# Output weights folded into each batch's key-value sums, and a query that is normalised by token before it is turned

## What is computed

```python
x = x + attn_a(layernorm(x)); x = x + ffn(layernorm(x))
x = x + attn_b(layernorm(x)); x = x + ffn(layernorm(x))

def attn_a(x):                                 # linear attention, 16 heads of 16
    q = elu(x @ Wq + bq) + 1; k = elu(x @ Wk + bk) + 1; v = x @ Wv + bv
    kv  = einsum('bkhd,bkhm->bhdm', k, v)       # sums over a batch's 2048 tokens
    out = einsum('bqhd,bhdm->bqhm', q, kv)
    out = out / maximum(einsum('bqhd,bkhd->bqh', q, k), 1e-6)[..., None]
    return out @ Wo + bo
def ffn(x):
    return square(relu(x @ Ws1)) @ Ws2 + routed # routed is zero unless a weight bound fails
```

## Time and profile before

| | before |
|---|---|
| time, median of 3 runs | 434.23 us (433.89 to 434.29) |
| profiled execution, span | 432.7 us |
| TensorE busy | 416.6 us (96%) |
| VectorE busy | 316.3 us (73%) |
| ScalarE busy | 217.6 us (50%) |
| GpSimd busy | 217.1 us (50%) |

### The profile page before, as it was taken

The page is one execution under the profiler, slowest core; times in us unless marked ns, Lnnn a source line. Parts: engine busy times, 40 slices in busy tenths (PEclk is TensorE's granted clock), DMA queues, the critical chain, the costliest instruction groups (busy, mean ns, idle before and its releaser), DMA issues.

```text
span 432.7 us, 7753 instructions
## 1 busy us (share of the span) xinstructions
PE 416.6 (96%) x2570; PEld 345.7 (80%) x2570; DVE 316.3 (73%) x707; ACT 217.6 (50%) x383; POOL 217.1 (50%) x317
## 2 busy tenths in 40 slices
PE   8998999999999999899999999999999999999993
PEld 5787889988987988889788886787887787787862
DVE  6769977676668766647878887877778767787864
ACT  3766777778777775326434342343244324334341
POOL 3675776776677764031345336534516416514532
PEclk9999999999999999999999999999999999999998
DMA  8701221111100000300110111011001010011103
GB/s 264 245 7 46 57 88 54 51 49 48 48 0 0 2 2 1 101 0 6 51 52 20 36 51 52 2 51 50 21 31 35 18 52 27 26 51 50 50 4 106
DMA packets 22793, 20.59 MB, mean 48 GB/s; under 512 B 3271, under 2 KB 22733, under 8 KB 22733
## 3 DMA queue, kind: packets, MB, share of 16 engines
q1 hardware_dynamic: 22172, 19.32, 14.1%
q10 hardware_dynamic: 560, 0.52, 0.4%
HBM read 11.32 MB, written 8.45 MB: 46 GB/s over the span
## 4 chain that ended last, share of the span: by engine, by line
PE 68%; DVE 8%; ACT 7%; POOL 7%; issue 5%; SPq 2%; DMA 1%; DVEq 1%; POOLq 0%; ACTq 0%
PE PB L1462 7%; PE PT L1504 6%; PE PA L1462 6%; PE PB L1483 6%; PE PA L1538 4%; PE PA L1544 4%; PE PA L1539 3%; PE PT L1548 3%; PE PA L1473 3%; ACT scratch L568 3%; PE PB L1510 3%; POOL ln_rstd L441 2%; PE PG L1334 2%; POOL ln_rstd L439 2%; DVE ln_bn L800 2%
## 5 line engine op out<-in xcount | busy, mean ns | idle before, releaser
L491 POOL TENSOR_TENSOR ln_a<-ln_bn 128x4 f32<-128x4 f32 x32 | 6.5, 203 | 136.1 <-DVE ln_bn L1003 136.1
L463 POOL TENSOR_TENSOR xn_pair<-scratch,xn_pair 128x1024 fp32r<-128x1024 f32 x16 | 38.4, 2402 | 18.9 <-ACT xn_pair L579 18.9
L883 DVE SCALAR_TENSOR_TENSOR scratch<-scratch,PB 128x512 f32<-128x512 f32 x32 | 20.9, 684 | 36.4 <-ACT scratch L615 36.3
L1003 DVE BATCH_NORM_STATS2 ln_bn<-x_all 128x6 f32<-128x256 f32 x128 | 44.9, 412 | 0.9
L568 ACT ACTIVATE scratch<-x_all,ln_shift,ln_rstd 128x255 f32 (+1 forms) x60 | 31.2, 593 | 22.6 <-POOL ln_shift L445 22.6
L452 POOL TENSOR_TENSOR x_all<-x_all,wvo 128x1024 f32 (+1 forms) x16 | 38.6, 2410 | 0.1
L452 POOL TENSOR_TENSOR x_all<-x_all,ob_rows 128x1024 f32<-128x1024 f32 x16 | 37.7, 2356 | 0.0
L1307 PE MATMUL PB<-wk_hi,xt_hi 128*128 128x256 f32 x128 | 36.9, 288 | 0.6 <-DVE xt_lo L828 0.4
L1309 PE MATMUL PB<-wk_hi,xt_lo 128*128 128x256 f32 x128 | 36.2, 283 | 0.0
L1308 PE MATMUL PB<-wk_lo,xt_hi 128*128 128x256 f32 x128 | 36.2, 283 | 0.0
L736 ACT ACTIVATE scratch<-PA,ln_rsq 128x256 f32<-128x256 f32 x30 | 12.6, 471 | 45.4 <-PE PA L1462 40.2
(11 more groups left out here) (247 smaller groups left out, 1139.0 us busy)
## 6 DMA issues: line engine op xcount, KB each, us to landing
x_all<-n_L_attn_a_inputs_q_dram SPq DMA_DIRECT2D x15, 512.0 KB, 3.5
out_dram<-x_all SPq DMA_DIRECT2D x15, 512.0 KB, 3.1
out_dram<-x_all SPq DMA_DIRECT2D x2, 256.0 KB, 2.2
x_all<-n_L_attn_a_inputs_q_dram ACTq DMA_DIRECT2D x2, 128.0 KB, 3.0
x_all<-n_L_attn_a_inputs_q_dram SPq DMA_DIRECT2D x2, 128.0 KB, 2.7
setup<-in_L_attn_a_Wk_dram SPq DMA_DIRECT2D x1, 256.0 KB, 4.6
setup<-in_L_attn_a_Wq_dram ACTq DMA_DIRECT2D x1, 256.0 KB, 5.0
wvo<-in_L_attn_a_Wv_dram SPq DMA_DIRECT2D x1, 256.0 KB, 6.7
```

Of the source, the lines that this page charges most:

```text
L463: nc.gpsimd.tensor_tensor(xn_pair[:, :, 1, :], xn[g % 2], xn_pair[:, :, 0, :].bitcast(F32), ALU.subtract).then_inc(x_lo, 1)
L1003: nc.vector.bn_stats(ln_bn[:, slot, t:t + 1, :], x_tile(n, t)).then_inc(bn, 1)
```

## The change

- The key-value sums of a batch, masked, are multiplied by Wo once per batch (m_product), and the result is split (m_hi, m_lo). These take the place of wo_hi and wo_lo in pass 2. The key sums of a batch are made as a row on all partitions (one matmul with a broadcast column).
- Queries are computed by token together with the keys: one product of 512 columns (kq) into two PSUM pairs, by halves of a group; q_all holds them by token. exp, features and roundings run by halves, statistics three groups ahead; the key sums times x are made of 256-column matmuls, by halves. The hardware loops are written out.
- In pass 2 GpSimd multiplies the query by the key sums (q_product, one step ahead, first in its step); VectorE reduces that by head, takes the maximum and the reciprocal, and multiplies the query in place (query). TensorE transposes this query where it transposed the attention. The product of query and key-value sums and the normalising from PSUM go away.
- ScalarE scales, and GpSimd adds, all four tiles of the second sum (two before), except in the last two groups. The variances of both sets are one series of five operations on GpSimd. The add of the down product is in halves. For the first group q_product and query stand inside the last group of pass 1. Part of the FFN's weight folding moves ahead of the last key sums.

The core of the diff:

```diff
@@ GpSimd
+            def q_product(j):
+                n, b = lagged(j // B, j % B, 0)[1:]
+                pool.wait_ge(ksum_done, b + 1)
+                pool.wait_ge(q_done, 2 * (n + 1))
+                if j == 0:
+                    pool.wait_ge(t1_mm, NG - 1)
+                else:
+                    pool.wait_ge(q_norm, 3 * (j - 1) + 1)
+                nc.gpsimd.tensor_tensor(prod.rearrange("p (t d) -> p t d", t=T), q_all[:, n * T:(n + 1) * T, :],
+                                        ksum[:, b:b + 1, :].to_broadcast([P, T, D]), ALU.mult).then_inc(q_prod, 1)
...
+            for n in range(NG):
+                x_low(n, 1)
+                if n == 0:
+                    pool.wait_ge(w2_loaded, 16 * 8)
+                if n == NG - 1:
+                    q_product(0)
+                add_bo(n)
+                if n + 3 < NG:
+                    rstd(n + 3)
+                if n + 1 < NG:
+                    x_low(n + 1, 0)
@@ GpSimd, the order of a step after the change
+                if i + 1 < NG:
+                    q_product(i + 1)
+                if runs(r) or runs(v):
+                    ge(pool, rsq, i - 1)
+                    variances(i, r, v)
                 if runs(r):
+                    pool.wait_ge(t2_mm, C * (r + 1))
                     add_row(nr, ob_rows, ob_added)
                 chain(i, 1)
+                if runs(v) and by_dve(v) < T:
+                    pool.wait_ge(f4_scaled, act_tiles(v + 1))
...
+                    last = x_all[:, nv * T + by_dve(v):(nv + 1) * T, :]
+                    nc.gpsimd.tensor_tensor(last, last, y3[:, by_dve(v):T, :], ALU.add).then_inc(out_pool, 1)
@@ VectorE
+            def query(j):
+                n = lagged(j // B, j % B, 0)[1]
+                by_head = q_all[:, n * T:(n + 1) * T, :].rearrange("p t (h e) -> p (t h) e", e=HD)
+                dve.wait_ge(q_prod, j + 1)
+                nc.vector.reduce_sum(norm_sb[:, :], prod.rearrange("p (k e) -> p k e", e=HD), AX).then_inc(q_norm, 1)
+                dve.wait_ge(q_norm, 3 * j + 1)
+                nc.vector.tensor_scalar(norm_sb[:, :], norm_sb[:, :], NORM_EPS, None, ALU.max).then_inc(q_norm, 1)
+                dve.wait_ge(q_norm, 3 * j + 2)
+                nc.vector.reciprocal(norm_inv[:, :], norm_sb[:, :]).then_inc(q_norm, 1)
+                dve.wait_ge(q_norm, 3 * j + 3)
+                nc.vector.tensor_tensor(by_head, by_head, norm_inv[:, :].unsqueeze(2).to_broadcast([P, T * H, HD]),
+                                        ALU.mult).then_inc(q_ready, 1)
...
+            for n in range(NG):
+                g, b = n % G, n // G
+                k_features(n, 0)
...
+                if n == NG - 1:
+                    query(0)
+                k_features(n, 1)
+                q_features(n, 1)
...
+                k_low(n, 1)
@@ VectorE, a step
                 if runs(i):
-                    regions = ((6, 2, PT[:, 1, 0:2 * KVW]), (0, 3, PB[:, 0, 0:3 * KVW]), (3, 3, PB[:, 1, 0:3 * KVW]))
-                    dve.wait_ge(o_mm, i + 1)
-                    for k0, nb, reg in regions:
-                        last = nc.vector.tensor_scalar(norm_sb[:, k0:k0 + nb, :], reg.rearrange("p (k w) -> p k w", w=KVW)[:, :, P:KVW],
-                                                       NORM_EPS, None, ALU.max)
-                    last.then_inc(o_norm, 1)
...
+                    for c in range(C):
+                        dve.wait_ge(o_hi_done, C * i + c + 1)
+                        ge(dve, w_mm, i)
+                        nc.vector.tensor_tensor(o_lo[:, c, :], PB[:, c, :], o_hi[:, c, :].bitcast(F32),
+                                                ALU.subtract).then_inc(o_lo_done, 1)
+                if runs(r) or runs(v):
+                    reciprocal_variances(i, r, v)
...
                 chain(i, 1)
+                if i + 1 < NG:
+                    query(i + 1)
...
                     nc.vector.tensor_tensor(h2s, h2, PT[:, 1, :], ALU.mult).then_inc(f1_scaled, 1)
...
+                    for h in range(2):
+                        dve.wait_ge(f2_mm, 2 * r + h + 1)
+                        nc.vector.tensor_tensor(pair(x_group(nr), h), four(PB)[:, 2 * h:2 * h + 2, :], pair(x_group(nr), h),
+                                                ALU.add).then_inc(f2_added, 1)
@@ TensorE
+            def m_product(b):
+                pe.wait_ge(kv_masked, C * (b + 1))
+                pe.wait_ge(ksum_done, b + 1)
+                for c in range(C):
+                    last = mm(PG[:, 1, c * D:(c + 1) * D], kvt[:, c, :], wo_raw[:, c, :], start=True, stop=True)
+                last.then_inc(m_mm, 1)
...
+                    kq(n, 0)
+                    g_product(n - 1, 1)
+                if n + 1 < NG:
+                    t1(n + 1)
...
+                    kq(n, 1)
...
+                g_product(n, 0)
+            fold_ffn()
+            g_product(NG - 1, 1)
@@ TensorE, a step
-                        last = mm(dst, q_all[:, (b * G + g) * C + c, t * P:(t + 1) * P], kv_all[:, b * C + c, :], start=True, stop=True)
-                    last.then_inc(o_mm, 1)
+                    pe.wait_ge(q_ready, i + 1)
+                    for c in range(C):
+                        ge(pe, f2_added, 2 * (i - 2) + c + 1)
+                        for t in range(T):
+                            last = nc.tensor.transpose(PB[:, c, t * P:(t + 1) * P], q_all[:, n * T + t, c * P:(c + 1) * P], ident[:, :])
+                        last.then_inc(ot_mm, 1)
...
                 if i == 0:
                     fold_ffn_product()
+                    kv_product(B - 1)
...
+                if i == 0:
+                    m_product(B - 1)
...
-                                mm(four(PA)[:, t, :], hi, wo_hi[:, c, :], start=(c == 0), stop=False)
-                                mm(four(PA)[:, t, :], hi, wo_lo[:, c, :], start=False, stop=False)
+                                mm(four(PA)[:, t, :], hi, m_hi[b][:, c, :], start=(c == 0), stop=False)
+                                mm(four(PA)[:, t, :], hi, m_lo[b][:, c, :], start=False, stop=False)
```

More of the change, by code:

```diff
@@ L318, in runs @@
         def runs(j):
[L320 to L325 removed]
+            return 0 <= j < NG
         @block.sync
@@ L759, in step @@
                 if i == 0:
+                    transposed_g(B - 1)
+                chain(i, 0)
+                if runs(v) and i < NG:
+                    scale_tiles(i, v)
+                chain(i, 1)
+                if i == 0:
                     fold_ffn_product()
@@ L1313, in q_product @@
-            def q_product(n, g, batch):
-                ge(pe, q_done, n)
-                for o in range(C):
-                    if batch is not None and o == C - 1:
-                        kv_product(batch)
-                    dst, cols = PA[:, o, :], slice(o * P, (o + 1) * P)
-                    for c in range(C):
-                        hi, lo = xt_hi[:, c, :], xt_lo[:, c, :]
-                        mm(dst, wq_hi[:, c, cols], hi, start=(c == 0), stop=False)
-                        mm(dst, wq_hi[:, c, cols], lo, start=False, stop=False)
-                        last = mm(dst, wq_lo[:, c, cols], hi, start=False, stop=(c == C - 1))
-                    last.then_inc(q_mm, 1)
@@ new lines, in fold_ffn @@
+            def fold_ffn():
+                pe.wait_ge(w2_loaded, 16 * 8)
+                pe.wait_ge(q_done, 2 * NG - 1)
+                for c in range(C):
+                    mm(PA[:, 0, 0:F], ones_f[:, :], ws1[:, c, :], start=(c == 0), stop=(c == C - 1))
+                for c in range(C):
+                    nc.tensor.transpose(PA[:, 0, (1 + c) * F:(2 + c) * F], ws2[:, c * P:(c + 1) * P], ident[:, :])
+                for c in range(C):
+                    last = nc.tensor.transpose(PA[:, 1, c * P:(c + 1) * P], ob_rows[:, c * P:(c + 1) * P], ident[:, :])
+                last.then_inc(fold_mm, 1)
@@ new lines, in _ @@
+            for n in range(NG):
+                g, b = n % G, n // G
+                if n == 0:
+                    first_kq()
+                else:
+                    kq(n, 0)
+                    g_product(n - 1, 1)
+                if n + 1 < NG:
+                    t1(n + 1)
+                if g == 0 and b > 0:
+                    g_transposes(b - 1)
+                if g == 1 and b > 0:
+                    m_product(b - 1)
+                if n > 0:
+                    kq(n, 1)
+                if g == 0 and b > 0:
+                    kv_product(b - 1)
+                elif n == 0:
+                    pe.wait_ge(flag_ready, 1)
+                g_product(n, 0)
```

702 lines of the change are left out of this document (318 added, 384 removed).

## The result

| | before | after |
|---|---|---|
| time, median | 434.23 us (5 runs) | 469.14 us (468.64 to 471.40, 5 runs) |
| ratio after to before | | 1.082 (1.079 to 1.085) |
| profiled execution: time, span | span 432.7 us | 471.4 us, span 469.7 us |
| TensorE busy | 416.6 us | 409.0 us |
| VectorE busy | 316.3 us | 377.6 us |

What follows compares the result with a forecast made beforehand. TensorE's matmuls bounded nearly everything before; after the change VectorE, held by GpSimd, was to bound the second pass. 434.2 − 0.6 (first pass) + 2.0 (turn, with step 1) + 11.2 (steps 2 to 15) = 446.8 us, range 421 to 462.

Steps and rivals of the forecast that it cites:

- The bound: Second pass: VectorE, held by GpSimd's operations, sets a plain step at 13.2 us where TensorE would allow 11.3.
- The plain step: Second-pass step without side work: 13.2 us against 13.45 before, its maximum and multiply held by GpSimd's adds.
- First pass: First pass, TensorE: merged product and left-out copies gain slightly more than new matmuls cost, −0.6 us (bounds −6 and +4).
- The fourth rival: First pass: the merged product runs at the shorter matmul spacing, giving 409 us; chance 0.02.
- The turn: Between the passes: normalising the first query delays the last sums; step 1 starts +3.4 us, step 2 +2.0.
- Steps with side work: Second pass, steps 2 to 15: small-attention work ahead of the query makes the maximum and multiply wait, +11.2 us in sum.
- the four kinds of step: Second pass, per step: 3, 4, 14, 15 at 13.4 us; 2, 5, 9, 13 at 16.3; 6, 7, 10, 12 at 18.9; 8, 11 at 15.
- the second rival: Second pass: GpSimd keeps the port between operations, so plain-step multiplies also wait for the query product; 459 to 475 us; chance 0.08.
- The first rival: Second pass: the multiply is ready ahead of GpSimd's add, which waits; plain steps 12.25, time 422 us (415 to 429); chance 0.28.

Runs made afterwards that it cites:

- TensorE kept busy: Kernel after with 14 to 46 extra matmuls (results unused) in seven steps while TensorE waits for the gate product: 456.14 us, ratio to before 1.052.
- the better version: Kernel after with all normalisers in PSUM, step 2's two small operations at the step's end, 38 extra matmuls: 423.98 us, ratio to before 0.978.

## Why the prediction was right and wrong

- **The bound.** Right: VectorE, held by GpSimd, takes TensorE's place. The plain step came out at 12.8 to 13.4 against 13.2, with a reduce of 1.22 (1.2), a held maximum, a reciprocal of 0.56 (0.55) and a multiply that ends one multiply after GpSimd's add; TensorE waits 1.4 us there, where 1.5 to 2 were forecast. The normaliser in PSUM shows the cause. The Trainium skill ("SBUF — State Buffer", section Who interferes with whom) says that a tensor-scalar in the two-port form and a GpSimd operation exclude each other; the trace agrees for the 64-element form, which no row of before showed: 0.79 us from SBUF, 0.23 from PSUM.
- **First pass.** −0.6 forecast; the last key product starts at 169.91, against 170.12 for the last query product before. Nothing gained, as worked out; from run to run this point moves by 1.5 us, so no more can be said. The fourth rival, shorter spacing of the merged product, did not occur.
- **The turn**, +3.4 forecast, +9.2 measured. The step that failed: after the bias add I let the multiply run freely to 175.0; it ended at 178.1, 3.1 us later. Of these, 1.5 are the bias add, which ended at 174.75 and not at 173.3, since the query product ahead of it started later and took 2.85. The other 1.6 are a hold that the walk lacks: the second query's product was queued right behind the bias add and held the multiply to 177.05, where from 175.42 it would have ended at 176.5. Some 2 us more are the lower clock (twelve matmuls in 2.7 for 1.44 us, the transposes in 1.79 for 1.04). That its place was to blame also fell: moved behind the sums it costs the same.
- **Steps with side work**, +11.2 forecast, +30.1 measured. The prediction gave them 5 us either way; they were 18.7 us off. The second step that failed, and the larger one, is the price of a wait of TensorE, taken at its length alone. Of the 18.7 us some 14.5 are this term that the sum lacked: in seven steps TensorE waits 2.7 to 6.9 us, the clock behind the wait is the lower one, and the second up product takes 1.45 to 2.08 us for 1.12, the down product up to 3.8 for 1.9 (the waits of 1.4 in plain steps left the clock at 1.00). The rest, some 4 us (228.6 with TensorE kept busy against 224.4), is mis-sized holds. With TensorE kept busy the four kinds of step take 52.9, 69.9, 75.7 and 30.1 against 53.6, 65.2, 75.6 and 30.0 forecast, so the miss lies in steps 2, 5 and 13: the side work's own small operations are held as well (step 2: a copy of 2.25 and a product of 2.37 in a row; step 5: 2.26), which I had taken at their durations beside other queues, and in step 5 the waiting maximum was passed over by the query product. In step 6 the multiply was passed over in the same way (4.70).
- **The rivals.** The time lies in the second rival's 459 to 475, but not by its mechanism: in plain steps the multiply goes ahead of the query product each time. So that the range of the second rival holds it is luck. The first rival's order of operations appears when the maximum is left out, at 444.57 us and not at 415 to 429, since other steps stay held. That the better version lies there has other causes: nothing is held, two operations moved, and extra matmuls keep the clock up.
- **The range** was too narrow at its upper end, since no case had the clock in it: every row of before showed 1.00, so the price of a wait of TensorE was taken as the wait alone.

## What to carry over

Before work is moved from TensorE to VectorE and GpSimd, list for every VectorE operation whether it reads two operands from SBUF or copies or scales from SBUF to SBUF, and which GpSimd operation is queued at that moment; a small intermediate in PSUM can free a whole chain (36 us here, by an edit of a few lines). A wait that TensorE didn't have before can cost more than its length (13 us here): look at the granted clock behind it, count what it does there at half pace, and try extra matmuls in the wait. Do the walk through each kind of step, not through the plain one alone.

## What the runs showed of the hardware beyond this

- A GpSimd power did not hold to its end: a maximum that arrived at 355.52 under the power of 354.74 to 357.65 ended at 357.24 (VectorE and GpSimd in step 10 of the kernel after):

```profile
354.74 2.91 POOL L554 TENSOR_TENSOR raw_b<-raw_b,minus_half 64x16 f32<-64x16 f32 x1
...
355.52 1.72 DVE L951 TENSOR_SCALAR norm_sb<-norm_sb 128x64 f32<-128x64 f32 x1
```

In step 6 a maximum that arrived as far into the power (286.15, power from 285.37 to 288.28) took 0.19 us and was not held at all.

- A multiply of two SBUF operands ran beside GpSimd's clearing, a maximum from SBUF to SBUF did not. In step 7 (add to 308.59, clearing 308.54 to 309.16) the multiply ends at 309.74, 1.15 after the add, about its usual length; in step 5 the maximum sat through the clearing (264.45 to 265.08). The same section of the Trainium skill says that the second operand uses the shared way for reading alone; these rows agree.

```profile
306.22 2.37 POOL L581 TENSOR_TENSOR x_all<-x_all,scratch 128x1024 f32<-128x1024 f32 x1
...
306.38 3.36 DVE L955 TENSOR_TENSOR q_all<-q_all,norm_inv 128x1024 f32<-128x1024 f32 x1
...
308.54 0.62 POOL L548 MEMSET q_all<- 128x640 f32 x1
```

- The one that waits can be GpSimd: where the multiply went first, the query product took 3.36 us for 2.4.
